# A two-layer graph network on one core: VectorE works on three groups at once in layer 0, and layer 1's comparisons read and write one row of 640 numbers

## The reference

```
h = x @ W ;  e = leaky_relu(h[src]·att_src + h[dst]·att_dst, 0.2)
e = exp(e - segment_max(e, dst)[dst]) ;  alpha = e / segment_sum(e, dst)[dst]
x = layernorm(x + tanh(segment_sum(h[src] * alpha, dst) + bias))     # layer 0
h = gelu(x @ W_pre + b_pre) ;  aggr = segment_sum(h[src] * edge_attr, dst)
z = x + aggr ;  x = layernorm(x + z + gelu(gelu(z @ W1 + b1) @ W2 + b2))   # layer 1
```

## Time and profile before

| | |
|---|---|
| median of three runs | 3724.72 us |
| the profiled execution's own span | 3722.8 us |
| GpSimd busy | 2781.1 us, 75% |
| VectorE busy | 2438.3 us, 65% |
| TensorE matmul busy | 2393.6 us, 64% |
| ScalarE busy | 1283.2 us, 34% |
| layer 0's last gather starts, layer 1's first | 1960.21 us, 1988.88 us |

### The profile page before, as it was taken

How to read it: one execution, slowest core, us unless ns; L and a number is a source line. 1 busy time by engine, 2 the same in 40 slices (tenths; PEclk the granted TensorE clock), 3 DMA queues, 4 the chain that set the end, 5 groups by cost and what they waited for, 6 DMA issues and landing times.

```text
span 3722.8 us, 66966 instructions
## 1 busy us (share of the span) xinstructions
PE 2393.6 (64%) x16704; PEld 1951.7 (52%) x16705; DVE 2438.3 (65%) x6240; ACT 1283.2 (34%) x3893; POOL 2781.1 (75%) x2950
## 2 busy tenths in 40 slices
PE   6433343434344444444445988989888989999888
PEld 3333333333333333333334777777776777777776
DVE  7444444444466666566666777777777788888886
ACT  5433343434445555555553111111111221111222
POOL 7777777777777777777775777777777777777776
PEclk7555555555555555555557999999999999999998
DMA  5222221222222222222223343443334343444332
GB/s 102 43 42 42 41 44 42 44 42 43 42 43 44 43 44 43 43 44 45 44 45 99 93 94 90 95 94 94 95 91 96 93 96 91 97 95 99 93 95 70
DMA packets 351632, 254.26 MB, mean 68 GB/s; under 512 B 254125, under 2 KB 279218, under 8 KB 351387
## 3 DMA queue, kind: packets, MB, share of 16 engines
q0 software_dynamic: 94016, 146.16, 17.8%
q1 hardware_dynamic: 242753, 99.71, 11.7%
q10 hardware_dynamic: 14618, 6.14, 0.6%
HBM read 244.43 MB, written 7.25 MB: 68 GB/s over the span
## 4 chain that ended last, share of the span: by engine, by line
POOL 60%; issue 24%; ACT 4%; DVE 4%; PE 3%; DMA 2%; ACTq 1%; DVEq 1%; POOLq 0%; SPq 0%
POOL rows L690 60%; ACT onehot L747 1%; DMA rows<-table,src_i 1%; DMA src_i<-in_src_dram 1%; PE bank L1086 1%; ACT L790 1%; ACTq L740 0%; ACT pair L767 0%; DVE score L1361 0%; PE bank L1029 0%; PE bank L962 0%; ACT rowu L796 0%; DVE bst L1399 0%; ACT unused L790 0%; DVE newp L1352 0%
## 5 line engine op out<-in xcount | busy, mean ns | idle before, releaser
L690 POOL DMA_INDIRECT rows<-table,src_i x2850 | 2694.8, 946 | 896.0 <-issue 859.5
L1086 PE MATMUL bank<-node,hot 128*128 128x288 bf16 x9310 | 1228.4, 294 | 28.1 <-issue 16.5
L995 PE MATMUL bank<-onehot,rows 128*97 128x72 f32 (+1 forms) x3048 | 584.9, 369 | 814.9 <-ACT onehot L777 814.9
L1086 PEld LDWEIGHTS bank<-node,hot 128*128 128x128 bf16 x9310 | 932.2, 101 | 282.4 <-issue 20.9
L995 PEld LDWEIGHTS bank<-onehot,rows 128*97 128x97 f32 x3048 | 530.8, 281 | 854.4 <-issue 792.5
L1505 DVE TENSOR_SCALAR hot<-node,key 128x642 bf16<-128x642 int16 x1862 | 870.3, 539 | 130.8 <-PE bank L1086 80.0
L900 ACT ACTIVATE pair<-dst_i 128x8 f32<-128x8 int32 x196 | 35.2, 180 | 1175.3 <-DVE rows L1531 904.3
L747 ACT ACTIVATE onehot<-iota,far_dst 128x72 f32 (+1 forms) x1564 | 384.4, 328 | 23.0
L1339 DVE SCALAR_TENSOR_TENSOR other<-onehot,bank 128x576 f32<-128x576 f32 (+1 forms) x196 | 121.9, 622 | 404.1 <-ACT bank L760 335.4
L1073 PE MATMUL bank<-onehot,rows 128*96 128x40 f32 (+1 forms) x3128 | 306.8, 256 | 88.4 <-DVE rows L1536 50.6
L1073 PEld LDWEIGHTS bank<-onehot,rows 128*96 128x96 f32 x3128 | 295.8, 170 | 110.1 <-issue 88.7
(11 more groups left out here) (204 smaller groups left out, 1931.1 us busy)
## 6 DMA issues: line engine op xcount, KB each, us to landing
attr<-in_edge_attr_dram SPq DMA_DIRECT2D x190, 336.0 KB
rows<-table,src_i POOLq DMA_INDIRECT x2850
node<-in_src_dram SPq DMA_DIRECT2D x195, 64.0 KB
attr<-in_edge_attr_dram SPq DMA_DIRECT2D x190, 48.0 KB
dst_i<-in_dst_dram SPq DMA_DIRECT2D x200, 4.0 KB
src_i<-in_src_dram SPq DMA_DIRECT2D x195, 4.0 KB
src_i<-in_src_dram SPq DMA_DIRECT2D x190, 3.5 KB
dst_i<-in_dst_dram SPq DMA_DIRECT2D x190, 3.5 KB
```

Of the source, the lines that this page charges most:

```text
L690: pool.indirect_dma_start(rows[:, u, j * width:(j + 1) * width], None, table, bass.IndirectOffsetOnAxis(ap=src_i[:, u, j:j + 1], axis=0))\
L995: last = pe.matmul(total[:, 0:w], rows0(u, it)[:, j, 0:D1], wide(weights, w)[:, j, :], start=j == 0, stop=j == most - 1)
L1086: last = pe.matmul(p_got[t], hot[:, c % HOTS, i, t * P:(t + 1) * P], tab[:, a, :, :].rearrange("p k d -> p (k d)"), start=a == 0, stop=a = ...
```

## The change

In layer 0, VectorE's work on a group is cut in two. `started` (1339, 1309 and 1344 of before) is done for group g+2 at the end of `attend(g)`; the bending `bent` and the largest node value `top_node` are done for group g+1 within `attend(g)`. `score` gets one buffer per slot, laid over the attribute buffers that layer 0 doesn't use. ScalarE's order follows: exponentials of g, `given` and `sloped` of g+2, `away` of g+3, and `away` now writes into the single buffer `other` and so waits for the `shift` of the group before. TensorE sums a group's eight tiles in one piece and does its part of a middle chunk after it, not within it. SyncE and GpSimd wait for `e0.acc`, which TensorE raises after its sum, instead of `e0.free`. In layer 1, `src16` and the first 640 numbers of `hot` are one row each.

The diff, cut to its core:

```diff
-        score = sb("score", [P, TILES * WIN])
+        further_score = sb("further_score", [P, TILES * WIN])
...
+        score = attr[:, :, :].rearrange("p s n -> p (s n)")[:, 0:SLOTS * TILES * WIN].rearrange("p (u n) -> p u n", u=SLOTS)
+        further_other = attr[:, SLOTS - 1, 0:TILES * WIN]
...
-        src16 = node[:, at_src16:at_got].bitcast(INT16).rearrange("p (r e) -> p r e", r=3)
+        src16 = node[:, at_src16:at_got].bitcast(INT16)[:, 0:BOOKED * P]
...
+        def later(g, it, u, k):
+
+            if it is ROUNDS or (it is ROUNDS - 1 and u + k > SLOTS):
+                return None
+            return g + k, it + (u + k) // SLOTS, (u + k) % SLOTS
...
-                    sp.wait_ge(e.free, g + 1)
+                    sp.wait_ge(e0.acc if e is e0 else e1.free, g + 1)
...
+                act.wait_ge(t0.shift, g + 1)
                 for j in range(tiles_of(g)):
-                    last = act.activation(wide(onehot[:, u, :], w)[:, j, :], iota[:, bass.ds(lo, w)], ACT.Square,
+                    last = act.activation(wide(other, w)[:, j, :], iota[:, bass.ds(lo, w)], ACT.Square,
                                           scale=FAR, bias=far_dst[:, u, j:j + 1])
                 last.then_inc(t0.away, 1)
...
+            def sloped(g, it, u, w):
+
+                act.wait_ge(t0.shift, g + 2)
+                act.activation(p_slope(w, tiles_of(g)), by_half(score[:, u, :], w, tiles_of(g)), ACT.Copy, scale=SLOPE)\
+                    .then_inc(t0.slope, 1)
...
             def weights(g, it, u, ws):
                 w = ws[0]
-                if g is not LAST and u > 0:
-                    away(g + 1, it + (u + 1) // SLOTS, (u + 1) % SLOTS, ws[1])
...
                 act.wait_ge(t0.newp, g + 1)
                 act.activation(p_newp[:, 0:w], newp[:, 0:w], ACT.Copy).then_inc(t0.newpb, 1)
-                if g is not LAST:
-                    if u < SLOTS - 1:
-                        given(g + 1, it, u + 1, ws[1])
...
                 act.wait_ge(t0.score, g + 1)
                 act.activation(fade[:, u, 0:w], drop[:, 0:w], ACT.Exp)
-                act.activation(onehot[:, u, 0:tiles_of(g) * w], score[:, 0:tiles_of(g) * w], ACT.Exp).then_inc(t0.w, 1)
...
+                        act.activation(onehot_x[:, 0:TILES * w], further_score[:, 0:TILES * w], ACT.Exp).then_inc(tx.w, 1)
+                if later(g, it, u, 2):
+                    given(*later(g, it, u, 2), ws[2])
+                    sloped(*later(g, it, u, 2), ws[2])
+                if later(g, it, u, 3):
+                    away(*later(g, it, u, 3), ws[3])
...
                 w = ws[0]
+                if later(g, it, u, 1):
+                    spread_top(t0, g + 2, ws[1], top_diag, p_topb)
...
                 pe.wait_ge(e0.free, g + SLOTS)
-                if g is LAST:
-                    window_sum(p_acc0, onehot[:, u, :], it, u, range(LAST_T), w, LAST_T).then_inc(e0.acc, 1)
-                    return
-                window_sum(p_acc0, onehot[:, u, :], it, u, range(TILES // 2), w)
-                if u == SLOTS - 1:
-                    due(pe, it, middle)
-                spread_top(t0, g + 2, ws[1])
-                window_sum(p_acc0, onehot[:, u, :], it, u, range(TILES // 2, TILES), w).then_inc(e0.acc, 1)
+                window_sum(p_acc0, onehot[:, u, :], it, u, range(tiles_of(g)), w, tiles_of(g)).then_inc(e0.acc, 1)
+                if later(g, it, u, 2):
+                    turn_top(t0, g + 3)
+
+            def middle_due(it):
+                due(pe, it, middle)
...
+            def started(st, g, it, u, w):
+
+                v.wait_ge(t0.away, g + 1)
+                v.wait_ge(t0.given, g + 1)
+                n = tiles_of(g)
+                st.link(v.scalar_tensor_tensor(wide(other, w, n), wide(other, w, n), -1.0,
+                                               over_window(p_src, w, n), ALU.mult, ALU.add))
+                largest(t0, other, w, n)
+                v.tensor_tensor(wide(score[:, u, :], w, n), wide(other, w, n), over_tiles(p_dst[:, 0:w], w, n), ALU.add)\
+                    .then_inc(t0.shift, 1)
+
+            def bent(st, g, it, u, w):
+
+                n = tiles_of(g)
+                v.wait_ge(t0.slope, g + 1)
+                st.step(v.tensor_tensor(by_half(score[:, u, :], w, n), by_half(score[:, u, :], w, n), p_slope(w, n), ALU.max))
...
             def attend(g, it, u, ws):
                 w = ws[0]
                 lo, further, prev = window(u, "0_" + named(it, u, ws))
-                st = Steps(v, e0.v, g * STEPS0, STEPS0)
-                v.wait_ge(t0.away, g + 1)
-                v.wait_ge(t0.given, g + 1)
+                st = Steps(v, e0.v, AHEAD0 + g * STEPS0, STEPS0)
                 here = bass.ds(lo, w)
                 n = tiles_of(g)
-                st.link(v.scalar_tensor_tensor(wide(other, w, n), wide(onehot[:, u, :], w, n), -1.0,
-                                               over_window(p_src, w, n), ALU.mult, ALU.add))
-                largest(t0, w, n)
+                candidate(st, t0, g + 1, here, w, p_topb)
+                v.tensor_tensor(newp[:, 0:w], cand[:, 0:w], peak[:, here], ALU.max).then_inc(t0.newp, 1)
                 after = None if g is LAST else load_window(g + 1)
+                v.wait_ge(t0.newp, g + 1)
                 v.wait_ge(t0.w, g + 1)
-                v.tensor_tensor(wide(score, w, n), wide(other, w, n), over_tiles(p_dst[:, 0:w], w, n), ALU.add)\
-                    .then_inc(t0.shift, 1)
-                if first(it) and u < SLOTS - 1:
-                    score_column(u + 1)
-                top_node(st, t0, g + 1, w)
-                v.wait_ge(t0.slope, g + 1)
-                st.step(v.tensor_tensor(by_half(score, w, n), by_half(score, w, n), p_slope(w, n), ALU.max))
-                candidate(st, t0, g + 1, here, w)
-                v.tensor_tensor(newp[:, 0:w], cand[:, 0:w], peak[:, here], ALU.max).then_inc(t0.newp, 1)
-                v.wait_ge(t0.newp, g + 1)
                 st.step(v.tensor_tensor(drop[:, 0:w], peak[0:D1, here], newp[0:D1, 0:w], ALU.subtract))
+                if later(g, it, u, 1):
+                    bent(st, *later(g, it, u, 1), ws[1])
+                else:
+                    st.skip()
+                v.wait_ge(t0.newpb, g + 1)
+                v.tensor_tensor(wide(score[:, u, :], w, n), wide(score[:, u, :], w, n), over_tiles(p_newp[:, 0:w], w, n),
+                                ALU.subtract).then_inc(t0.score, 1)
+                st.wait()
+                st.step(v.tensor_tensor(peak[:, here], cand[:, 0:w], peak[:, here], ALU.max))
 
...
+                v.wait_ge(e0.free, g + SLOTS - 1)
                 st.link(v.tensor_tensor(acc[:, before_here], acc[:, before_here], fade[:, (u - 1) % SLOTS, 0:w], ALU.mult))
-                v.wait_ge(e0.acc, g + 1)
-                v.tensor_tensor(acc[:, before_here], acc[:, before_here], p_acc0[:, 0:w], ALU.add).then_inc(e0.free, 1)
-                v.wait_ge(t0.newpb, g + 1)
-                v.tensor_tensor(wide(score, w, n), wide(score, w, n), over_tiles(p_newp[:, 0:w], w, n), ALU.subtract)\
-                    .then_inc(t0.score, 1)
-                st.step(v.tensor_tensor(peak[:, here], cand[:, 0:w], peak[:, here], ALU.max))
-                st.done()
+                v.wait_ge(e0.acc, g + SLOTS)
+                v.tensor_tensor(acc[:, before_here], acc[:, before_here], p_acc0[:, 0:w], ALU.add)\
+                    .then_inc(e0.free, 1)
+                if later(g, it, u, 1):
+                    top_node(st, t0, g + 2, ws[1], top_diag)
+                else:
+                    st.skip()
...
+                if later(g, it, u, 2):
+                    if first(it) and u + 2 < SLOTS:
+                        score_column(u + 2)
+                    started(st, *later(g, it, u, 2), ws[2])
+                else:
+                    st.skip()
+                st.done()
...
                 for i, a in enumerate(range(PIECE[c], PIECE[c + 1])):
-                    last = v.tensor_scalar(hot[:, c % HOTS, i, :].rearrange("p (r e) -> p r e", r=3),
-                                           src16[:, :, 0:ROW3], key[:, a:a + 1], None, ALU.is_equal)
+                    last = v.tensor_scalar(hot[:, c % HOTS, i, 0:BOOKED * P], src16, key[:, a:a + 1], None, ALU.is_equal)
                 last.then_inc(g_hot, 1)
```

More of the change, by code:

```diff
@@ L664, in body @@
                         pool.wait_ge(s_last, 16)
-                        pool.wait_ge(e.free, LAST + 1)
+                        pool.wait_ge(e0.acc if e is e0 else e1.free, LAST + 1)
                         for j in range(LAST_T):
@@ L783, in weights @@
                         act.activation(fade_x[:, 0:w], drop[:, 0:w], ACT.Exp)
-                        act.activation(onehot_x[:, 0:TILES * w], score[:, 0:TILES * w], ACT.Exp).then_inc(tx.w, 1)
-                if u == SLOTS - 1 and it is not ROUNDS - 1:
-                    away(g + 2, it + 1, 1, ws[2])
```

(37 more changed lines are left out.)

51 lines of the change are left out of this document (29 added, 22 removed).

## The result

The changed kernel takes 3754.18 us (median of four runs, 3753.48 to 3756.0), the kernel before 3724.95 us, measured beside it: a ratio of 1.0078, 95% interval 1.0064 to 1.0092. The profiled execution has a span of 3751.7 us.

What follows compares the result with a forecast made beforehand. GpSimd's gathers were taken to bound both layers. The span of 3722.8 plus 0 (layer 0's body), 5 (seam) and 36 (layer 1's gathers) gave 3763.8, with 1.9 around it 3766 us; range 3728 to 3870.

Steps and rivals of the forecast that it cites:

- A: Layer 1: gathers get longer beside the new comparisons; 3766 us, own range 3738 to 3810, chance 0.66.
- a longer wait for the table: Sign at the seam between the layers: GpSimd's wait for the table 33 us, not 27.7.
- rival C: Layer 1: a gather waits until the whole piece of comparisons is over; 258 us more, 3990 us, chance 0.16.
- B: Layer 1: gathers don't lose, only the seam is left; 3730 us, range 3724 to 3733, chance 0.14.
- D: Seam between the layers shrinks by 3 to 8 us, gathers losing nothing; 3717 to 3722 us, chance 0.04.
- Layer 1's gathers: Layer 1: gathers wait for two-port comparisons in flight, 304 pieces at 0.12 us, +36 us; bounds 0 to 176.
- the mean loss at a meeting: Layer 1: 0.10 us at a piece's first gather start, 0.03 or so at the next, 0.12 us a piece.
- What is left less 0.13 us: Layer 1: a gather waits for about what is left of the VectorE instruction in flight less 0.13 us.
- The seam: Between the layers: the last groups' exponentials end later, so layer 1 starts later; +5 us, from 0 to +9.
- The cycle: Layer 0, a group when VectorE is behind after a middle chunk: 7.9 us, under GpSimd's 10 us a group.
- Layer 0's body: Layer 0: GpSimd stays the bound and no slot comes free too late; 0 us.
- Elsewhere the slack is 2.5 to 5 us: Layer 0, slots behind a middle chunk where the next group has eight gathers: 2.5 to 5 us to spare, cost 0.

Runs made afterwards that it cites:

- r1: Changed kernel with layer 1's comparisons put back as three rows of 214 numbers: 3743.47 us, ratio 1.0050 to the kernel before.
- r2: Kernel before with only layer 1's comparisons changed to one row of 640 numbers: 3734.35 us, ratio 1.0024.
- e4: Kernel before with layer 1's comparisons reading two rows of 320 numbers at a distance of 322: comparisons 382 ns; whole time not usable.
- e2: Kernel before with layer 1's comparisons as one row of 640 numbers, first run: comparisons 366 to 608 ns; whole time not usable.
- q3: Kernel before with each layer 1 comparison as two instructions of 320 numbers: 3789.79 us, ratio 1.0174.
- r5: Kernel of r1 with ScalarE's distances written to the group's slot of onehot and issued between given and sloped: 3728.94 us, ratio 1.0007.

## Why the prediction was right, and where its terms were off

**What held.** GpSimd's gathers bound both layers, and 266 us of VectorE's busy time were worth nothing. The likeliest case, A, came: comparisons with a least length of 366 ns (0.36 was taken), stretched to 635 beside gathers; 515 meetings (490 were taken); longer gathers in layer 1 with no wait between them; a longer wait for the table. r1 and r2 show the two halves apart. The rule from the Trainium skill's page SBUF — State Buffer, Who interferes with whom, is borne out in both directions by the same rows, and e4 and the kernel before fit the form on which it depends. What a meeting costs, and whom, is not in that rule: the 43 gathers that met a comparison with over 0.3 us left lost 3 ns. In the changed kernel rival C's starving gathers stayed away, though e2 and e4 show that comparisons of this form can bring them about; B and D are ruled out by the longer gathers and the longer seam.

**Layer 1's gathers, forecast +36, measured +10.5.** The term that failed is the mean loss at a meeting: 0.12 us a piece was taken, 10.5 / 304 = 0.035 came. I had what is left of the comparison spread evenly at the first meeting. In fact 201 of the 284 first meetings found 0.1 to 0.2 us left, where nearly nothing is lost, and so did all 231 later ones: the two are in step at most first meetings too, not only at the second. In 128 of the 201 the gather before had already held up an earlier comparison of the run, as told above. "What is left less 0.13 us" holds for the 38 with 0.2 to 0.3 us (a mean of 0.26 left, 0.13 lost), but not as a general rule: the 43 with more left lost nothing, and q3's gathers lost far more.

**The seam, forecast +5, measured +11.2.** The cycle was taken as 7.9 us and is 8.2. The larger error is the chunk's place: I had ScalarE load its first table at 1933.6, from the landing of group 191's rows, as if nothing were left over from the chunk before. It loaded it at 1945.05. Of these 11.5 us, 7.5 are the later gathers, which belong to layer 0's body below. 3.6 are the backlog: group 191 is taken up 6.1 us after its last gather's start (1938.93), not 2.5. With 8.2 us a group instead of 7.5, a delay of 13 to 16 us isn't gone in five groups.

**Layer 0's body, forecast 0, measured +7.6.** The same step. "Elsewhere the slack is 2.5 to 5 us" was right for a chunk that finds no delay and wrong for the second of two in a row; group 10's wait has no chunk ahead of it and wasn't followed further. In the same sum TensorE's part was taken as 1.6 us and is 2.88 for the 16 matmuls of a group (L1016 at 1940.06). "Were I 3 us off, the 15 chunks would cost up to 15" was the bound, and 6.6 lies in it.

Both errors on the one side (+13.8) and the one on the other (-25.5) make the 11.8 us by which the forecast was high. That the total came nearer than its terms is luck: the errors have separate causes, and they happened to lie on opposite sides.

## What to carry to other kernels

When one engine must keep up with another, ask not whether its cycle is below the other's, but how many cycles lie between two interruptions: 10 us of arrival less 8.2 of work gives back 1.8 us a group, so five groups give back 9 us, and a 12 us interruption every five groups is then never paid back. A shorter instruction on an engine that isn't the bound can be the dearer one, if its form makes the bounding engine wait; look whether its length varies beside that engine, and whether the long form's did not. Before moving a block of work earlier, write down what each of its engines still has queued ahead of it.

## What the runs showed of the hardware that was not expected

- A gather can be held up over a whole run of comparisons in the fast form: 2.79 us over 12 halves, and once 8.40 us over two runs and the two-input operations between them (1513, 1516), where 0.94 is usual. Whole comparisons of 640 numbers do it too, more rarely: 2.10 us in e2 and up to 3.43 in e4, but at most 1.62 us in all of the changed kernel's layer 1. The two-input operations of layer 1's first round seem to hold gathers up as well: r5, whose comparisons are in the quiet form, has one gather of 2.23 us, and it starts at 2040.03 together with the first of two of them in a row.
- Half the numbers cost far more than half the time: 282 ns at least for 320, 366 for 640, so by these two about 0.2 us of each is fixed (an estimate). In the slower form 642 take 526.
- A gap between rows doesn't end the fast form: two rows of 320 with a gap have it (382 ns), three of 214 with a gap don't (539 ns).
- A gather holds up the comparison that runs into it until about 0.15 us after the gather's end, and so sets the place at which the next gather meets the run: 432 of 515 meetings cost the gather 9 ns each.
